# A transformer kernel with a new order for its first tile, stores in halves, and both value products in one place

## The reference

```python
q, k, v = heads(ln(x) @ Wq.T + bq), heads(ctx @ Wk.T + bk), heads(ctx @ Wv.T + bv)
logits = einsum('bhqd,bhkd->bhqk', q, k) / sqrt(32) + causal      # causal mask over 256 x 77
x = x + merge(softmax(logits) @ v) @ Wo.T + bo
h = silu(tlin(ln(x), w1_w, w1_s)) * tlin(ln(x), w2_w, w2_s)       # 256 -> 1024; tlin: (x @ w.T) * s
h = gelu(tlin(h, h1_w, h1_s))                                     # 1024 -> 1024
h = gelu(tlin(h, h2_w, h2_s))                                     # 1024 -> 1024
out = x + tlin(h, w3_w, w3_s)                                     # 1024 -> 256
```

## Time and profile before

| what | us |
|---|---|
| median of 3 runs | 1649.64 (1648.93 to 1652.39) |
| the profiled execution, time | 1654.17 |
| the profiled execution, span of the trace | 1652.4 |
| first product of the feed-forward part starts at | 69.34 |
| from one pass to the next | 99.92 |
| last product of the feed-forward part starts at | 1645.66 |

### The profile page before, as it was taken

One profiled execution on the slowest core, in us unless ns is written; L12 is line 12 of the kernel. 1 busy time (PEld: TensorE's weight loads), 2 busy tenths in 40 slices (PEclk: granted clock), 3 DMA queues, 4 the chain that ended last, 5 costly groups with the idle time before them and its releaser, 6 DMA issues.

```text
span 1652.4 us, 22285 instructions
## 1 busy us (share of the span) xinstructions
PE 1618.1 (98%) x9042; PEld 1321.1 (80%) x9042; DVE 786.3 (48%) x1245; ACT 736.9 (45%) x1099; POOL 125.3 (8%) x136
## 2 busy tenths in 40 slices
PE   6799999999999999999999999999999999999998
PEld 4688888888888888888888888888888878888887
DVE  5364634537354364634537354364534646345331
ACT  5653534436354353534435344353533535344342
POOL 1001010010100101001010100101001010100000
PEclk8799999999999999999999999999999999999999
DMA  9601000000100001000010100001000010000000
GB/s 385 244 5 39 13 29 25 29 13 13 42 13 29 25 4 38 13 29 25 4 38 13 40 15 29 13 13 42 13 29 25 4 38 13 29 26 1 13 0 14
DMA packets 18661, 58.88 MB, mean 36 GB/s; under 512 B 5456, under 2 KB 7632, under 8 KB 15824
## 3 DMA queue, kind: packets, MB, share of 16 engines
q1 hardware_dynamic: 18640, 58.57, 9.7%
HBM read 38.59 MB, written 8.45 MB: 28 GB/s over the span
## 4 chain that ended last, share of the span: by engine, by line
PE 95%; DVE 3%; issue 1%; ACT 1%; DMA 0%; POOL 0%; POOLq 0%; SPq 0%; ACTq 0%; DVEq 0%
PE ffn_banks L354 77%; PE att_banks L507 4%; PE att_banks L526 3%; PE att_banks L475 3%; PE att_banks L516 2%; PE att_banks L492 2%; PE att_banks L463 2%; PE att_banks L457 1%; PE att_banks L534 1%; DVE probs L721 1%; DVE a_lo L695 1%; DMA w_att_sb<-in_w_att 0%; DVE xln L649 0%; DVE a_f L690 0%; PE att_banks L449 0%
## 5 line engine op out<-in xcount | busy, mean ns | idle before, releaser
L354 PE MATMUL ffn_banks<-a_hi,h_sb 128*128 128x512 f32 x1024 | 407.9, 398 | 0.0
L354 PE MATMUL ffn_banks<-b_hi,h_sb 128*128 128x512 f32 x1024 | 399.7, 390 | 0.0
L354 PE MATMUL ffn_banks<-a_lo,h_sb 128*128 128x512 f32 x1024 | 399.6, 390 | 0.0
L354 PE MATMUL ffn_banks<-b_lo,h_sb 128*128 128x512 f32 x1024 | 398.5, 389 | 0.0
L354 PEld LDWEIGHTS ffn_banks<-a_hi,h_sb 128*128 128x128 f32 x1024 | 192.3, 188 | 45.0 <-issue 6.2
L701 DVE TENSOR_TENSOR b_lo<-b_f,b_hi 128x512 fp32r<-128x512 f32 x128 | 87.2, 691 | 292.2 <-ACT b_hi L580 292.2
L354 PEld LDWEIGHTS ffn_banks<-b_lo,h_sb 128*128 128x128 f32 x1024 | 192.3, 188 | 39.5
L354 PEld LDWEIGHTS ffn_banks<-b_hi,h_sb 128*128 128x128 f32 x1024 | 192.2, 188 | 39.4
L354 PEld LDWEIGHTS ffn_banks<-a_lo,h_sb 128*128 128x128 f32 x1024 | 192.5, 188 | 38.6
L579 ACT ACTIVATE a_f<-ffn_banks,vec 128x512 f32<-128x512 f32 x128 | 88.3, 690 | 301.7 <-PE ffn_banks L354 301.7
L701 DVE TENSOR_TENSOR a_lo<-a_f,a_hi 128x512 fp32r<-128x512 f32 x128 | 94.5, 738 | 258.6 <-ACT a_hi L580 258.6
(11 more groups left out here) (92 smaller groups left out, 1782.2 us busy)
## 6 DMA issues: line engine op xcount, KB each, us to landing
h_bits<-in_h SPq DMA_DIRECT2D x8, 1024.0 KB, 20.9
h_sb<-h_bits SPq DMA_DIRECT2D x8, 1024.0 KB, 5.4
out<-out_sb SPq DMA_DIRECT2D x16, 512.0 KB, 2.6
x_in<-in_x SPq DMA_DIRECT2D x15, 512.0 KB, 3.5
ln_t<-in_x_t SPq DMA_DIRECT2D x14, 512.0 KB, 4.3
ln_rows<-ln_rows_dram SPq DMA_DIRECT2D x14, 512.0 KB, 3.7
w_bits<-in_w SPq DMA_DIRECT2D x3, 1024.0 KB, 11.4
w_sb<-w_bits SPq DMA_DIRECT2D x3, 1024.0 KB, 25.5
```

Source lines behind the costliest of these rows:

```text
L354: mm = nc.tensor.matmul(psum, left, right, start=(k == 0 and part == 0), stop=(k == rows - 1 and part == 1))
```

## The change

**1. The first tile.** `FIRST` is written anew. The query projection of tile 1 (`Q` 0, 1) moves from before the first `PT` to behind `O`; the second `EXP` now comes before the copy of `T1` 1 on ACT. `PT` 0 to 3 come before `PV` 0 and 1. Four of the eleven checks go to DVE (`DVE_CHECKS`), as a maximum over 128x2048 16-bit numbers. The pieces are written onto themselves at one place, `KEEP`, at the end of SP's list, once all have arrived. The first `BIAS` waits for the first `MASK`, the second for the end of `LN2A`. There are 7 + 20 + 3 + 3 + 3 + 2 spins, and 4 behind the flag's product, where there were 8 + 4 + 4 and 4 ahead of it.

The diff, cut to its core:

```diff
+ACT_CHECKS = (0, 1, 2, 3, 4, 5, 7)
+DVE_CHECKS = (6, 8, 9, 10)
...
-    ("L1", 0), ("S", 0), ("L1", 1), ("MASK", 0), ("L1", 2), ...
+    ("L1", 0), ("S", 0), ("MASK", 0), ("L1", 1), ("L1", 2), ...
-    ("L2", 2), ("PT", 0), ("PT", 1), ("L2", 3), ("PV", 0), ("PT", 2), ("L2", 4), ("PT", 3),
-    ("L2", 5), ("PV", 1), ("L2", 6), ("O", 0), ("CTX", 0), ("L2", 7),
+    ("L2", 2), ("PT", 0), ("PT", 1), ("L2", 3), ("PT", 2), ("PT", 3), ("L2", 4), ("PV", 0), ("PV", 1),
+    ("L2", 5), ("L2", 6), ("O", 0), ("CTX", 0), ("L2", 7),
...
+    ("S", 0, 0), ("MASK", 0, 0), ("MAX", 0, 0), ("CHECK", 0, 0), ("S", 1, 0), ("SUB", 0, 0), ("SPIN", 7, 0),
+    ("MASK", 1, 0), ("MAX", 1, 0), ("CHECK", 1, 0), ("EXP", 0, 0), ("SUB", 1, 0), ("CHECK", 2, 0), ("EXP", 1, 0),
+    ("T1", 0, 1), ("SPIN", 20, 0), ("BIAS", 0, 0), ("SOFT", 0, 0), ("SOFT", 1, 0),
+    ("PT", 0, 0), ("PT", 1, 0), ("SPIN", 3, 0), ("CHECK", 6, 0),
+    ("PT", 2, 0), ("PT", 3, 0), ("SPIN", 3, 0), ("PV", 0, 0), ("PV", 1, 0), ("CTX", 0, 1), ("SPIN", 3, 0), ("CHECK", 3, 0),
+    ("CHECK", 8, 0), ("O", 0, 0), ("CHECK", 4, 0), ("CHECK", 9, 0), ("CHECK", 5, 0), ("Q", 0, 1), ("ADD", 0, 0), ("LN2S", 0, 0),
+    ("K", 0, 1), ("V", 0, 1), ("CHECK", 10, 0), ("CHECK", 7, 0), ("LN2A", 0, 0), ("BIAS", 0, 1), ("COUNT", 0, 0), ("VADD", 0, 1),
+    ("SPIN", 2, 0), ("T2", 0, 0), ("FLAG", 0, 0), ("KEEP", 0, 0),
...
+                    if step == "KEEP":
+                        for c in range(NP):
+                            sp.wait_ge(piece_loaded[c], 16)
+                        for c in range(NP):
+                            keep_piece(c)
...
+                    if step == "L4":
+                        half = slice(2 * n, 2 * n + 2)
+                        sp.wait_ge(out_ready, 2 * f + n + 3)
...
+                        sp.dma_start(dst[:, half, :], out_sb[:, half, :]).then_inc(stored, 16)
...
+                        if n == 2:
+                            pe.wait_ge(pt_act_done, NQ * t + 2)
+                            pe.wait_ge(pt_dve_done, NQ * t + 2)
+                        pair = (2, 0, 2, 0)[n]
...
+                        if n == 2 and f is not None:
+                            act.wait_ge(stored, 32 * f + 32)
...
+                        if a is None:
+                            half = slice(2 * n, 2 * n + 2)
+                            dve.wait_ge(out_scaled, 2 * f + n + 3)
...
+                            nc.vector.tensor_tensor(out_sb[:, half, :], out_sb[:, half, :], x1_keep[:, half, :], ALU.add)\
+                                .then_inc(out_ready, 1)
...
+                        pool.wait_ge(masked, 1)
...
+                        pool.wait_ge(ln_ready[1], 1)
```

More of the change, by code:

```diff
@@ L46 @@
 CHUNK = 2048
+ACT_CHECKS = (0, 1, 2, 3, 4, 5, 7)
+DVE_CHECKS = (6, 8, 9, 10)
 ORDER = [
-    ("L1", 0), ("S", 0), ("L1", 1), ("MASK", 0), ("L1", 2), ("MAX", 0), ("S", 1), ("L1", 3), ("SUB", 0),
+    ("L1", 0), ("S", 0), ("MASK", 0), ("L1", 1), ("L1", 2), ("MAX", 0), ("S", 1), ("L1", 3), ("SUB", 0),
     ("L1", 4), ("L1", 5), ("L1", 6), ("L1", 7), ("L1E", 0),
     ("EXP", 0), ("MASK", 1), ("MAX", 1), ("SUB", 1), ("EXP", 1), ("SOFT", 0), ("L2", 0), ("SOFT", 1), ("L2", 1),
[2 rows of a table removed]
[2 rows of a table added]
     ("L3", 0), ("LN2S", 0), ("L3", 1), ("L3", 2), ("LN2A", 0), ("LN1S", 0), ("L3", 3), ("L3", 4), ("ROWS", 0),
@@ L72 @@
 FIRST = [
[L73 to L79, removed]
+    ("K", 0, 0), ("T1", 0, 0), ("V", 0, 0), ("LN1S", 0, 1), ("Q", 0, 0), ("XLN", 0, 1),
+    ("S", 0, 0), ("MASK", 0, 0), ("MAX", 0, 0), ("CHECK", 0, 0), ("S", 1, 0), ("SUB", 0, 0), ("SPIN", 7, 0),
[6 more added lines that the diff above has]
+    ("SPIN", 2, 0), ("T2", 0, 0), ("FLAG", 0, 0), ("KEEP", 0, 0),
 ]
@@ L293, in keep_piece @@
             def keep_piece(c):
-                sp.wait_ge(checked, c + 1)
+                checks = DVE_CHECKS if c in DVE_CHECKS else ACT_CHECKS
+                sp.wait_ge(dve_checked if c in DVE_CHECKS else act_checked, checks.index(c) + 1)
                 sp.dma_start(pieces[c][2].bitcast(F32), pieces[c][1]).then_inc(pieces[c][3], 16)
@@ L537, in one_pass @@
                         spin(n)
+                    if step == "FLAG":
+                        pe.wait_ge(row_summed, 1)
+                        nc.tensor.matmul(fb[0:1, 0, 0:1], inexact_row[:], ones[:], start=True, stop=True).then_inc(flag_summed, 1)
+                        spin(4)
             pe.wait_ge(id_ready, 1)
@@ L556, in one_pass @@
                 for step, n, t in steps(f, a, b):
[L557 removed]
+                    if step == "CHECK" and n in ACT_CHECKS:
                         act.wait_ge(piece_loaded[n], 16)
+                        i = ACT_CHECKS.index(n)
                         nc.scalar.activation(junk[n][:].bitcast(mybir.dt.bfloat16), low_halves(n), ACT.Copy,
[L560 removed]
+                                             accum_out=inexact[:, i:i + 1]).then_inc(act_checked, 1)
                     if step == "L1":
@@ L677, in one_pass @@
                 for step, n, t in steps(f, a, b):
+                    if step == "CHECK" and n in DVE_CHECKS:
+                        dve.wait_ge(piece_loaded[n], 16)
+                        i = len(ACT_CHECKS) + DVE_CHECKS.index(n)
+                        nc.vector.tensor_reduce(inexact[:, i:i + 1], low_halves(n), AX_X, ALU.max).then_inc(dve_checked, 1)
                     if step == "COUNT":
-                        dve.wait_ge(checked, NP)
+                        dve.wait_ge(act_checked, len(ACT_CHECKS))
+                        dve.wait_ge(dve_checked, len(DVE_CHECKS))
                         nc.vector.tensor_reduce(inexact_max[:], inexact[:], AX_X, ALU.max).then_inc(max_checked, 1)
@@ L712, in one_pass @@
                                               ab[:, 1, :].rearrange("p (j q) -> p j q", j=NQ)).then_inc(t1_dve_done, 1)
-                    if step == "V":
+                    if (step == "V" and (f is not None or t == 0)) or step == "VADD":
                         dve.wait_ge(v_ready, t + 1)
@@ L819, in one_pass @@
                         pool.wait_ge(x1_done, 1)
+                        pool.wait_ge(ln_ready[1], 1)
                         add_bias(x1_keep[:])
-                    if step == "L4":
+                    if step == "L4" and a is not None:
                         half = slice(2 * n, 2 * n + 2)
```

66 lines of the change are left out of this document (32 added, 34 removed).

## The result

The changed kernel takes 1626.57 us, the median of 4 runs (1626.35 to 1627.77), against 1651.02 (1648.93 to 1654.29, 4 runs) for the kernel before: a ratio of 0.985, 95% interval 0.983 to 0.987. The forecast was 1625.6, in a range from 1618.5 to 1633.

The account below looks back on a forecast made before the run. PE was taken as the bound, 95% of the chain. Gains of 6.3 (scores), 2.3 (values), 14.2 (first tile) and 1.2 (end), 24.0 in all, took 1654.17 to 1630.2; less 4.53 gave 1625.6 us, range 1618.5 to 1633.

Parts of the forecast that it names:

- The bound and the scores: PE bounds the kernel; in the loop, the earlier mask removes PE's wait of 0.42 a pass, 6.3 us in all.
- The cover: In the loop, the mask moved ahead ends 0.4 us before DVE's `L1` 1 can start, so it costs nothing.
- the slower case: In the loop, DVE's mask waits on ACT's copy, queued behind POOL's addition: 1650 to 1660 us, chance 0.03.
- The values: In the loop, from first `PT` to `O`, three excursions instead of four save 0.15 a pass, 2.3 us.
- the bound of 4: Largest gain allowed for joining transposes and value products in the loop: 0.27 a pass, 4 us in all.
- The first tile until `O`: First tile, following DVE's list: `O` starts at 39.15 instead of 49.14, 10.0 us less.
- The bound of 1.2: First tile: `CHECK` 6 on DVE would take 1.2 us if 16-bit numbers went through at twice the rate.
- the rival of 4.6: First tile: DVE's checks take 4.6 instead of 2.3 us each, 7.6 us in all, giving 1633; chance 0.08.
- From `O` on: First tile: `O` 2.55 shorter, stretch to `LN2A` 0.4 longer, `LN2A` 1.5 and `T2` to first feed-forward product 0.55 shorter.
- The clock: Rival: PE's clock falls to half in the first tile, costing 4.5 us as the middle, giving 1630; chance 0.15.
- The end: End of kernel: DVE's addition of 0.7 replaces POOL's 1.26, half-size last transfer saves 0.6; 1.2 us less.
- The offset of 4.53: Whole kernel: the profiled execution lay 4.53 us above the median before; the same was taken off the forecast.

Follow-up runs that it names:

- `mask_alone`: The kernel before with only the mask of batch 0 moved one place earlier in the loop; 1645.9 us, ratio 0.9962.
- `pv_apart`: The changed kernel with its two value products apart again, the four transpositions still together; 1631.57 us, ratio 0.9883.
- `t2_beside_k`: The changed kernel with the passes' `T2` moved behind the last piece of `L3`, next to the projections; 1627.77 us, ratio 0.985.
- `spins_ends`: The changed kernel with 18 instead of 12 spins at the start and 10 instead of 4 behind the flag's product; 1623.62 us, ratio 0.9833.
- `no_spins`: The changed kernel without the 38 spins of its first tile; 1628.11 us in one run.
- `checks_on_act`: The changed kernel with all eleven checks on ACT and three more buffers for what ACT writes; 1630.14 us in one run.
- `bias_early`: The changed kernel without POOL's two new waits; 1630.18 us in one run.

## Why the prediction was right, step by step

**The bound and the scores.** Right: 0.45 a pass alone in `mask_alone`, against 0.42. The cover held; in the changed kernel DVE's mask ends at 855.63, 0.36 before the evacuation that follows it starts, and nothing of the slower case, the queue from POOL over ACT to the mask, is in the trace.

**The values.** The sign was right, the size not: 0.38 a pass where 0.15 was put, 5.7 in all instead of 2.3 and beyond the bound of 4. The step that failed is "0.53 is left for four excursions from the feed-forward products and back, 0.13 each". The 0.53 is not spread over four. 0.27 of it (3.90 less 16 products at 0.227) stands behind one value product, 0.16 behind the other, and a group of transpositions fewer gives nothing (`pv_apart`, `t2_beside_k`). The rows for it were there before the change: sixteen products took 3.64 behind one kind of group and 3.90 behind the other. A residue was divided by a count where it should have been read group by group. The bound missed 0.14 besides, since two value products of 1.00 need 1.86 when they stand together.

**The first tile until `O`.** Right. `O` at 39.15 was forecast; it came at 40.88 after a start 2 us late, and at 38.82 in `spins_ends`. `XLN` took 1.38 as put. `SUB` was read rightly: begun at 22.38, held while POOL works until 23.37, done at 24.67. `CHECK` 6, for which no row stood, took 2.28 against 2.3: 2048 16-bit numbers in 2.28 are no faster each than 1232 of 32 bits in 1.44, so the maximum has no double rate here. The bound of 1.2 and the rival of 4.6 both fall.

**From `O` on.** `O` 3.55, gain 2.45 against 2.55. From its end to `LN2A` 5.21 (49.64 less 44.43) against 5.45, `LN2A` 1.38 as put. `T2` to the first feed-forward product 5.43 (56.52 less 51.09) instead of 6.22: 0.8 against 0.55; `COUNT`'s two instructions started at 51.54 and 51.74, took 0.17 and 0.15, and were not held by the second `BIAS`, which ran from 51.16. All told the first feed-forward product came 14.9 earlier with an undisturbed start (54.47) against 14.2; in the profiled execution 12.8. The chain runs over PE from `O` to `T2`, but DVE ends `LN2A` at 51.02 and `T2` starts at 51.09, so the two are as tight as was put down.

**The clock.** This rival came true in some executions, and in the changed kernel without its price. PE's idle stretches were as forecast: 1.72 ahead of the second scores in every execution with this first tile, and 1.62 ahead of `T1` where the clock stayed up. In the profiled execution of the changed kernel the clock fell to 0.50 from 22.4 to 25.8. In that of `pv_apart`, with the same steps, it was at 1.00 until 55.3; this window of `pv_apart` lies where the fall would be, 2.1 earlier:

```profile
20.00:22.00 2.00, 1.81 (x18) 1.62 (x14) 1.97 (x2) 1.89 (x2) 1.28 (x1) 1.00 0.97 406
```

Both took 44.33 from the second projection to the first feed-forward product. So the fall cost nothing: it hit `T1` and spins with room behind them. `no_spins` (1.75 on `O`) and `checks_on_act` (0.9 ahead of `PT` 0) show what it costs where there is none. The Trainium skill, page "TensorE: Matmul & The Clock Gate", Part 1, has the clock follow how busy PE has been lately; what decided between the two executions no run here shows. The prediction had read too short an idle stretch for the kernel before, 17.4 to 19.6. PE stood until 20.23, and the clock fell within that stretch, so the 1.6 and 1.7 were weighed against 2.2 where it was 2.86:

```profile
20.23 2.01 PE L492 MATMUL att_banks<-k_t,q_t 32*128 32x77 f32 x32 [2.86 <-DVE probs L721]
```

The forecast that the clock would be 1.00 from 23 on was wrong for the profiled execution; that it would be so from 26 and through `O` was right. Two things were not in the sum. One is the start of the profiled execution, 2.0 lost, 0.55 of it by the later weights and 1.5 by the half clock. The other is the first scores and the products ahead of them, which gained 0.65 since the clock was back sooner. PE's pause there was not shorter (3.15, before 2.21), but before the change the clock had been half since 64.0, and now it fell only at 56.5. How long it then stays half differs from run to run (3.4 after the restart here, 4.3 in `pv_apart`, 9.6 in `bias_early`), so the 0.65 is no sure gain.

**The end.** 0.6 instead of 1.2. The end of the changed kernel, in DVE's and SP's timeline:

```profile
1619.96 0.69 DVE L732 TENSOR_TENSOR out_sb<-ffn_banks,vec 128x512 f32<-128x512 f32 x1 [2.42 <-PE ffn_banks L366]
...
1621.40 0.33 SPq L334 DMA_DIRECT2D out<-out_sb  x1
```

DVE's first instruction to the store's issue takes 1.44; before it was 2.06, with POOL's addition of 1.26 in it: 0.62 less, as put down. The step that did not come out is "the last transfer is half as large, 0.26 MB less at 420 GB/s, 0.6". From the issue to the end of the span it is 4.36 before (1652.4 less 1648.04) and 4.40 now (1625.8 less 1621.40). But this pair does not price the transfer. The DMA view of the last 4 to 6 us, with the last store alone, KB and us from issue to landing, for the kernel before, the changed kernel and `spins_ends`:

```profile
out<-out_sb SPq DMA_DIRECT2D x1, 512.0 KB, 3.0
...
out<-out_sb SPq DMA_DIRECT2D x1, 256.0 KB, 4.0
...
out<-out_sb SPq DMA_DIRECT2D x1, 256.0 KB, 2.3
```

The same store of 256 KB lands after 4.0 and after 2.3. In the eight executions that have it the span ends 2.7 to 4.6 after its issue. Over all stores of a run the median until landing is 2.6 for 512 KB and 2.0 for 256 KB, just the 0.6 that was put. So the term may well be right, and a scatter of up to 1.9 in the last store hides it in a single execution. What sets the scatter is open.

**The offset of 4.53** between the profiled execution and the median was taken over unchanged. For the changed kernel it is 1.2, and with the fourth run of the kernel before it would have been 3.15 there. The forecast lands within 1 us of the result because this offset and the undervalued terms, 24.0 against 26.6, err against each other. The mechanism was right for the mask, the first tile and the addition at the end, and wrong for the values; that the forecast came within 1 us was luck.

## What to carry to other kernels

Price a move in TensorE's list by the row of what follows the group, not by the number of groups: put products of one form together where leaving that form shows as a longer row behind it, and leave alone those whose next row is not longer. An instruction of GpSimd that holds VectorE is best put beside a reduction, and it pays to ask which of its neighbours has slack before it is moved. In a stretch where TensorE waits for others, take out of its list what is not due, fill the gap with products that only keep the clock, and look in particular at the two ends of the stretch.

## What the runs showed of the hardware that was not expected

- Sixteen feed-forward products (128 x 128 loads) take 3.65 behind transpositions (128 x 77), and 3.89 to 3.90 behind scores (32 x 128) or value products (77 x 32); eight transpositions take 1.03 instead of 0.87 behind value products.
- In the profiled execution of the changed kernel the granted clock fell to half from 22.4 to 25.8, behind an idle stretch of 1.72 and 1.3 us of work. In `pv_apart`, with the same steps and the same idle 1.72, it stayed at full. The length of the last idle stretch alone does not decide.
- In two executions with the same instructions at the start the first projection began at 8.37 and at 7.82, and took 2.11 and 1.32; the clock was half in the first, after 2.05 of idle time, and full in the second, after 0.70. With 18 spins (36 rows) ahead instead of 12 it began at 8.26 and took 1.05.
- A store of 256 KB at the end of the kernel landed 2.3 to 4.2 us after its issue in eight executions; the median of all such stores in a run is 2.0.
- POOL's addition of 2.37 over 128x1024 held a subtraction on DVE (2.29 instead of 1.44) and a layer norm (3.33 instead of 1.38), but not the maximum beside which it began (1.45).
